# Value products laid out by a table, with six exponentials kept and operands of four head duos

## The chip, the core and the metric

The kernel runs on one core of one Trainium2 chip. The metric is the device time of one execution in microseconds (us), lower is better. The five engines of the core run their own instruction lists in order and wait for each other by semaphores: TensorE (PE in the profile; PEld is its weight load), VectorE (DVE), ScalarE (ACT), GpSimd (POOL) and SyncE (SP, whose queue here only issues DMAs).

## What is computed

Two transformer blocks over x of 8 batches, 1024 rows and 128 channels. Block 0 has one attention head over 1024 rows and a mixture of 8 experts; block 1 has 16 heads of 8 channels and a feed-forward of 512. The change touches the attention of block 1 alone:

```python
def _L1_attn_ref(x, Wq, Wk, Wv, Wout, bout):
    HEADS = 16
    b, n, c = x.shape
    m = HEADS
    d = Wq.shape[0] // m
    q = jnp.einsum('bnc,hc->bnh', x, Wq).reshape(b, n, m, d)
    k = jnp.einsum('bnc,hc->bnh', x, Wk).reshape(b, n, m, d)
    v = jnp.einsum('bnc,hc->bnh', x, Wv).reshape(b, n, m, d)
    scale = d ** (-0.25)
    weight = jnp.einsum('bimd,bjmd->bmij', q * scale, k * scale)
    weight = jax.nn.softmax(weight, axis=-1)
    a = jnp.einsum('bmij,bjmd->bimd', weight, v).reshape(b, n, m * d)
    return jnp.einsum('bnh,ch->bnc', a, Wout) + bout
```

Its 8 x 16 tables of 1024 x 1024 weights are the bulk of the work. Everything else (block 0, the projections, the feed-forward) is called side work here.

## The kernel before

**Units.** Heads go in duos (the code's `pair`): 64 duos, 8 a batch. A duo's tables are cut into `UNITS` = 16 units, each two heads x 128 x 512, which fill one of three PSUM buffers (`buffer`, two banks each). Every table is made twice. The max unit (`max_scores`, L652) has queries on the partitions; VectorE takes its row maxima (`row_max`, L1084). The exp unit (`exp_scores`, L662) has keys on the partitions and three more rows of weights that carry the negated row maxima; ScalarE takes its exponential into `p` (`exps`, L858). A value unit (`values`, L678) multiplies `p` by v: four fp32 products into four groups of 32 columns of `pv_psum`, which sums over the 16 units of a duo. Then ScalarE copies `pv_psum` to `o_sb` (`copy_values`, L864), SyncE writes it out (`values_out`, L1359), and the next duo's first value unit may begin.

**Half steps.** A loop over h, the half step, runs on every engine; there are 1024 with exponentials (128 a batch) and 32 ahead of them. In half step h TensorE fills exp unit h, then max unit h + 32 (`2 * LEAD`), then does value unit h - 2 (`VALUES_LAG`), and then the side stages that a planner (`lay_out`) put there. So each half step has one value unit, whatever else it holds:

```python
        for h in range(-2 * LEAD, PAIRS * UNITS + 2):
            if 0 <= h < PAIRS * UNITS:
                exp_scores(h)
            if h + 2 * LEAD < PAIRS * UNITS:
                max_scores(h + 2 * LEAD)
            if 0 <= h - VALUES_LAG < PAIRS * UNITS:
                values(h - VALUES_LAG)
```

**The ring of three buffers.** Exp and max units take the buffers in turn (exp h, max h + 32, exp h + 1, ...). Max unit h + 32 needs the buffer that exponential h - 1 read, and exp unit h needs that which row maximum h + 30 read. A fill therefore waits (`buffer_of`) if ScalarE or VectorE has not finished its unit of the half step or two before.

**Side work.** All side stages of the loop take turns in one PSUM bank, `side_psum`. A stage that fills it waits until ScalarE or VectorE has emptied it of the one before (`empty`). The planner's `WORK` and `ROOM` set how much side work a half step may get; many half steps have none. Stages that go through `tiled` (L444: block 0's `scores` and `times_v`, `moe`, `wg`, `qk1` and others) use groups of 32 columns as the value units do; transposes (L530, L497, L604) use the whole array; exp and max units use two groups of 64 rows.

**Stores in SBUF.** Four buffers `p`, so exponential n waits for value unit n - 4. The operands `q_ops`, `k_ops` have `SLOTS` = 3 slots of `GROUP` = 2 duos; SyncE loads a group 11 half steps (`LOAD_BEFORE`) before its first max unit, 8 DMAs of 96 KB at a time. The first group's `k_ops` come by ScalarE's queue (`fetch_operands(e, 0, 1)`).

Of the kernel before, what the change touches and what calls it, by code (L numbers as in the profile page):

```python
# [11 lines left out]
P = 128  # L12
# [7 lines left out]
BANK = 512  # L20
HALVES = N // BANK
QUARTER = BANK // 2

VALUES_LAG = 2
EPS = 1e-5
# [10 lines left out]
ROW_HALF = 64  # L36
GROUP = 2
GROUPS = HEADS // 2 // GROUP
SLOTS = 3
VW = DH + 1  # L40
# [44 lines left out]
def half_line(half):  # L85
# [10 lines left out]
    for w in range(2):  # L96
# [24 lines left out]
        "moe": 10, "qk1": 11, "v1": 11, "nm": 1, "w2T": 6, "wff_a": 10, "wff": 12, "wout_mm": 11, "channels_b": 6, "ffn": 11}  # L121
ROOM, ROOM_MOST = (13, 4), 18


# [82 lines left out]


class Side:

# [59 lines left out]
masks_out0 masks_out1 masks_in0 masks_in1 hm gexp0 gexp1 gp0 gp1 x2_0 x2_1 parts0 parts1  # L270
max_filled max_done exp_filled exp_done pv_done pv_copied attention_out operands0 operands1 operands2
nm nm_split maxima0 maxima1
# [3 lines left out]
def build(nc, ctx, x_in, Wq0, Wk0, Wvdown, Wvup, Wg, bg, We, be, c0, wmod0,  # L276
          Wq1, Wk1, Wv1, Wout, bout, W1, b1, W2, b2, c1, wmod1, consts, select, out):
    S = {name: ctx.enter_context(nc.semaphore(name)) for name in SEMAPHORES}
    first, plan, last = make_plan()
    side, before_steps = side_table(first, plan, last)  # L280
    unit_order, unit_at = unit_table()

    def sb(name, shape, dt=F32):
        return ctx.enter_context(nc.sbuf_tensor(name, shape, dt))
# [50 lines left out]
    v1 = [sb(f"v1_{i}", [P, T, HEADS, VW]) for i in range(2)]  # L335
    p_sb = [sb(f"p{i}", [P, 2, BANK]) for i in range(4)]
    mx = [sb(f"row_max{i}", [P, 2, T, HALVES]) for i in range(2)]
# [89 lines left out]
    def tensor_program():  # L427
# [238 lines left out]
        def values(n):  # L666
            pair, kb, half = n // (2 * T), n // 2 % T, n % 2
            b, hp = divmod(pair, HEADS // 2)
            if n % (2 * T) == 0:
                pe.wait_ge(S["pv_zero"], 1)  # L670
                pe.wait_ge(S["pv_copied"], pair)
                emptied("v1", b, 1)
                pe.wait_ge(S["v1_ones"], 2)
            pe.wait_ge(S["exp_done"], n + 1)
            for hh in range(2):
                for part in range(2):
                    q = 32 * (2 * hh + part)
                    m = e.matmul(pv_psum[q:q + VW, half * QUARTER:(half + 1) * QUARTER], v1[b % 2][:, kb, 2 * hp + hh, :],  # L678
                                 p_sb[n % 4][:, hh, part * QUARTER:(part + 1) * QUARTER], start=n % UNITS == 0, stop=n % UNITS == UNITS - 1)
            m.then_inc(S["pv_done"], 1)  # L680
# [9 lines left out]
        for h in range(-2 * LEAD, PAIRS * UNITS + 2):  # L690
            if 0 <= h < PAIRS * UNITS:
                exp_scores(h)
            if h + 2 * LEAD < PAIRS * UNITS:
                max_scores(h + 2 * LEAD)
            if 0 <= h - VALUES_LAG < PAIRS * UNITS:
                values(h - VALUES_LAG)
            for name, *at in plan.get(h, ()):
                if name in stages:
                    stages[name](*at)
# [5 lines left out]
    def scalar_program():  # L705
# [148 lines left out]
        def exps(n):  # L854
            if n >= 4:
                act.wait_ge(S["pv_done"], n - 3)
            act.wait_ge(S["exp_filled"], n + 1)
            e.activation(p_sb[n % 4][:, :, :], unit("exp", n)[0][:, :, :], ACT.Exp).then_inc(S["exp_done"], 1)  # L858

# [14 lines left out]
        for h in range(-2 * LEAD, PAIRS * UNITS + 2):  # L874
            if 0 <= h < PAIRS * UNITS:
                exps(h)
            if h > 1 and h % UNITS == 1:
                copy_values(h // UNITS - 1)
            for name, *at in plan.get(h, ()):
# [404 lines left out]
    def sync_program():  # L1284
# [119 lines left out]
        for h in range(-2 * LEAD, PAIRS * UNITS + 2):  # L1404
            g, within = divmod(h + 2 * LEAD + LOAD_BEFORE, UNITS * GROUP)
            if within == 0 and g < B * GROUPS:
                load_operands(g)
            if h > 1 and h % UNITS == 1:
                values_out(h // UNITS - 1)
            for name, *at in plan.get(h, ()):  # L1410
# [39 lines left out]
```

## Time and profile before

| what | value |
|---|---|
| median of 3 runs | 1938.29 us (1933.97 to 1938.5) |
| the profiled execution | 1939.49 us, its span 1938.2 us |
| TensorE busy | 1736.9 us, 90% of the span |
| VectorE busy | 1527.8 us, 79% |
| ScalarE busy | 1371.4 us, 71% |
| GpSimd busy | 742.8 us, 38% |
| loop from the first exp fill to the last | 214.44 to 1900.61 us |

Busy time is what instructions of an engine cover. A matmul's end is modelled, so matmuls of one engine overlap in the rows: the start of a row less the start of the row before is what the first one cost TensorE, and that is how the rows below are read. In them a row merges neighbouring instructions of one form (x2, x8), and the brackets at its end say how long the engine was idle before it and what it waited for.

### The profile page before, as it was taken

What the parts mean: (1) busy time and instruction counts of PE and PEld (TensorE: products, weight loads), DVE (VectorE), ACT (ScalarE), POOL (GpSimd) and SP (SyncE); (2) the same over time, 40 slices, a digit from 0 to 9 for tenths busy, and PEclk for the clock granted to TensorE, in tenths of its full rate; (3) what the DMA queues carried; (4) which work ended last, traced back from release to release, by engine and by line L of the source; (5) the groups of instructions that cost most, each with busy time, mean ns of one, the idle gap of its engine ahead of it and who ended that gap; (6) DMA issues with size and microseconds to landing.
All of it is one profiled execution on the core that took longest, in us unless ns stands there. A gap on an engine that the chain in (4) does not pass through costs nothing.

```text
span 1938.2 us, 57276 instructions
## 1 busy us (share of the span) xinstructions
PE 1736.9 (90%) x24606; PEld 692.3 (36%) x24606; DVE 1527.8 (79%) x2326; ACT 1371.4 (71%) x1826; POOL 742.8 (38%) x1154
## 2 busy tenths in 40 slices
PE   5675789999999999999999999999999999999994
PEld 3542332333433343343433343343433333222222
DVE  5546877888788887889878887889878887899952
ACT  2431467877788777877778777877788777787883
POOL 2451364325644265324744166333753255102011
PEclk8887799999999999999999999999999999999997
DMA  2012021112111222102211131102311121211101
GB/s 64 24 56 88 24 76 53 32 42 77 51 54 33 55 88 61 47 11 84 75 54 32 43 100 35 51 27 57 98 54 31 44 84 33 65 38 46 34 16 39
DMA packets 97325, 100.46 MB, mean 52 GB/s; under 512 B 11088, under 2 KB 81456, under 8 KB 97072
## 3 DMA queue, kind: packets, MB, share of 16 engines
q1 hardware_dynamic: 95224, 94.84, 16.5%
q8 instruction: 193, 3.16, 0.7%
q10 hardware_dynamic: 1848, 1.97, 0.3%
q14 instruction: 60, 0.49, 0.1%
HBM read 61.25 MB, written 34.73 MB: 50 GB/s over the span
## 4 chain that ended last, share of the span: by engine, by line
PE 55%; ACT 14%; DVE 14%; POOL 9%; issue 6%; DMA 1%; SPq 1%; ACTq 0%; POOLq 0%; DVEq 0%
PE pv_psum L678 17%; PE side_psum L444 14%; ACT p L858 9%; PE buffer L662 9%; PE buffer L652 8%; DVE row_max L1084 8%; PE side_psum L530 2%; POOL hm L1203 2%; PE side_psum L497 1%; PE buffer L444 1%; POOL xn_b L1116 1%; DVE st_f L905 1%; ACT o_sb L864 1%; DVE onehot L1022 1%; ACT s L780 1%
## 5 line engine op out<-in xcount | busy, mean ns | idle before, releaser
L1084 DVE TENSOR_REDUCE row_max<-buffer 128x2 f32<-128x1024 f32 x1024 | 1235.8, 1220 | 255.6 <-PE buffer L652 245.2
L858 ACT ACTIVATE p<-buffer 128x1024 f32<-128x1024 f32 x1024 | 1043.9, 1026 | 245.3 <-PE buffer L662 230.3
L678 PE MATMUL pv_psum<-p,v 128*9 128x256 f32 x8192 | 638.7, 384 | 5.2 <-ACT o_sb L864 2.3
L652 PE MATMUL buffer<-k_ops,q_ops 48*128 48x512 bf16 x2048 | 399.9, 388 | 62.1 <-ACT p L858 25.4
L662 PE MATMUL buffer<-q_ops,k_ops 51*128 51x512 bf16 x2048 | 402.7, 390 | 24.2 <-DVE row_max L1084 18.4
L678 PEld LDWEIGHTS pv_psum<-p,v 128*9 128x9 f32 x8192 | 121.7, 88 | 348.1 <-issue 319.6
L662 PEld LDWEIGHTS buffer<-q_ops,k_ops 51*128 51x128 bf16 x2048 | 98.4, 93 | 389.9 <-DVE row_max L1084 200.5
L1216 POOL TENSOR_SCALAR nm_parts<-nm 128x16 bf16<-128x16 f32 x64 | 13.3, 208 | 401.1 <-DVE nm L1033 400.0
L652 PEld LDWEIGHTS buffer<-k_ops,q_ops 48*128 48x128 bf16 x2048 | 99.8, 94 | 186.7 <-ACT p L858 143.8
L1203 POOL TENSOR_TENSOR hm<-masks,hT_f 128x1024 f32<-128x1024 bf16 x64 | 136.9, 2150 | 28.7 <-PE side_psum L444 26.6
L444 PE MATMUL side_psum<-we,hm 128*32 128x128 f32 x3648 | 122.1, 275 | 6.1 <-POOL hm L1203 6.1
L1180 POOL TENSOR_TENSOR s<-s,consts 128x128 f32<-128x128 f32 x64 | 29.4, 459 | 226.2 <-ACT s L774 225.4
L444 PEld LDWEIGHTS side_psum<-we,hm 128*32 128x32 f32 x3648 | 101.0, 111 | 24.3 <-POOL hm L1203 9.1
L1186 POOL TENSOR_SCALAR rest<-s 128x128 f32<-128x128 f32 (+7 forms) x48 | 102.9, 2143 | 4.2
L780 ACT ACTIVATE s<-s,nm 128x256 f32<-128x256 f32 (+3 forms) x64 | 55.3, 864 | 45.8 <-DVE nm L991 33.1
L1108 POOL TENSOR_SCALAR sm_f<-mv_f 128x4 f32<-128x4 f32 x32 | 6.7, 211 | 184.8 <-DVE mv_f L908 184.8
L444 PE MATMUL side_psum<-v,p0T 128*32 128x129 f32 x1944 | 69.6, 276 | 0.8 <-DVE x L996 0.4
L444 PE MATMUL side_psum<-hT,g 128*32 128x512 f32 (+3 forms) x616 | 65.1, 494 | 0.2 <-ACT s L774 0.2
L444 PEld LDWEIGHTS side_psum<-v,p0T 128*32 128x32 f32 x1944 | 56.9, 111 | 16.9 <-ACT p0T L787 1.6
L774 ACT COPY s<-side_psum 128x512 f32<-128x512 f32 (+3 forms) x77 | 36.8, 478 | 27.7 <-PE side_psum L444 27.0
L787 ACT COPY p0T<-side_psum 128x512 f32<-128x512 f32 (+3 forms) x85 | 43.8, 516 | 17.5 <-PE side_psum L530 14.4
L1116 POOL TENSOR_SCALAR xn_f<-x,sm_f 128x128 f32<-128x128 f32 x112 | 54.0, 496 | 4.3 <-POOL sm_f L1110 4.3
(241 smaller groups left out, 1692.0 us busy)
## 6 DMA issues: line engine op xcount, KB each, us to landing
masks<-masks_rows SPq DMA_DIRECT2D x16, 1024.0 KB, 6.0
q_ops<-products SPq DMA_DIRECT2D x128, 96.0 KB
k_ops<-products SPq DMA_DIRECT2D x124, 96.0 KB
products<-q_parts SPq DMA_DIRECT2D x16, 384.0 KB, 2.8
products<-k_parts SPq DMA_DIRECT2D x14, 384.0 KB, 3.1
attention<-o_sb SPq DMA_DIRECT2D x256, 18.0 KB
x<-in_L_attn_inputs SPq DMA_DIRECT2D x8, 512.0 KB, 4.0
products<-q_parts SPq DMA_DIRECT2D x16, 256.0 KB, 3.1
```

Of the source, the lines that this page charges most:

```text
L444: m = e.matmul(out[q:q + COLUMN_TILE, :], weight[:, q:q + COLUMN_TILE], moving, start=start, stop=stop)
L530: m = e.transpose(v[:, j * P:(j + 1) * P], s0[i % 2][:, k * P:(k + 1) * P], ident)
L652: m = e.matmul(buffer[:, hh, :], q_ops[rows_of(hh, K_MAX), slot, of, i * P:(i + 1) * P], k_ops[rows_of(hh, K_MAX), slot, of, halves(half)[ ...
L662: m = e.matmul(buffer[:, hh, :], k_ops[rows_of(hh, K_EXP), slot, of, kb * P:(kb + 1) * P], q_ops[rows_of(hh, K_EXP), slot, of, halves(half ...
L678: m = e.matmul(pv_psum[q:q + VW, half * QUARTER:(half + 1) * QUARTER], v1[b % 2][:, kb, 2 * hp + hh, :], p_sb[n % 4][:, hh, part * QUARTER ...
L780: e.activation(s[:, start:P + n], s[:, start:P + n], ACT.Exp, bias=nm0[:, i:i + 1]).then_inc(S["p0"], 1)
L787: e.copy(p0T[i % 2][:, some[0]:some[-1] + 1, :].rearrange("p k q -> p (k q)"), v[:, 0:len(some) * P]).then_inc(S["side_act"], 1)
L858: e.activation(p_sb[n % 4][:, :, :], unit("exp", n)[0][:, :, :], ACT.Exp).then_inc(S["exp_done"], 1)
L1084: e.tensor_reduce(mx[pair % 2][:, :, i, half], unit("max", n)[0][:, :, :], axis=AX.X, op=ALU.max).then_inc(S["max_done"], 1)
L1116: m = e.tensor_scalar(xn[:, t, :], src[:, t, :], sm[:, 0, t:t + 1], sm[:, 2, t:t + 1], ALU.add, ALU.mult)
L1186: e.tensor_scalar(rest[:, 0:n], s[:, P:P + n], 0.0, NEG, ALU.is_equal, ALU.mult).then_inc(S["masked"], 1)
L1203: e.tensor_tensor(hm[t % 2][:, :, :], masks[:, :, cols], hT_f[:, cols].unsqueeze(1).broadcast_to([C, EXPERTS, P]), op=ALU.mult).then_inc(S ...
```

## The change

The count of value units in a half step is no longer one. A new function, `value_table`, goes over the half steps once with the plan of side work and chooses 0, 1 or 2 value units for each, so that the sum of squares of TensorE's work is least. Its unit of work is four column-tiled products of 128 columns; a value unit counts 2, a change of tiling `SWITCH` = 0.9, and less than `LIGHT` = 4.8 counts as 4.8. Value unit n is done 2 to 5 half steps (`LAG`, `LAG_MOST`) after exponential n. Two units are not put together where the second opens a new duo. The copy of `pv_psum` and its DMAs follow the half step in which a duo's last value unit stands. `p` has six buffers. The operands have 4 slots of one duo each, and SyncE loads one duo (4 DMAs) every 16 half steps. The order of exp units, max units and side stages is unchanged.

The table has 234 half steps without a value unit, 560 with one and 232 with two.

```diff
-VALUES_LAG = 2
+KEPT, LAG, LAG_MOST = 6, 2, 5
-GROUP = 2
+GROUP = 1
-SLOTS = 3
+SLOTS = 4
+SWITCH, LIGHT = 0.9, 4.8
+def side_work(stage):
+    name, *at = stage
+    if name.startswith("times_v"):
+        return work(stage) / 3, True
+    if name == "scores":
+        return chunks(at[1])[at[2]][1] / P, True
+    if name in ("channels", "channels_b", "transpose_p", "w2T"):
+        return 2.3, False
+    if name in ("nm", "onehotT"):
+        return 0.6, True
+    return (4, True) if name.endswith("_a") or name in EMPTIED_BY else (0, True)
+def value_table(plan):
+    total = PAIRS * UNITS
+    best = {0: (0.0, ())}
+    states = []
+    for h in range(total + LAG):
+        some = [side_work(s) for s in plan.get(h, ())]
+        inside, outside = sum(w for w, tiled in some if tiled), sum(w for w, tiled in some if not tiled)
+        new = {}
+        for left, (cost, at) in best.items():
+            for count in range(3):
+                now = left + (h < total) - count
+                done = min(h + 1, total) - now
+                if not max(0, min(LAG, total + LAG - 1 - h)) <= now + max(0, LAG - 1 - h) or now > LAG_MOST or done - count < 0:
+                    continue
+                if count == 2 and (done - 1) % UNITS == 0:
+                    continue
+                load = inside + outside + 2 * count + SWITCH * ((count > 0 or inside > 0) + (outside > 0))
+                sums = cost + max(load, LIGHT) ** 2
+                if now not in new or sums < new[now][0]:
+                    new[now] = (sums, left, count)
...
+    values_at = value_table(plan)
+    copied_at = {h: units[-1] // UNITS for h, units in values_at.items() if units and units[-1] % UNITS == UNITS - 1}
-    p_sb = [sb(f"p{i}", [P, 2, BANK]) for i in range(4)]
+    p_sb = [sb(f"p{i}", [P, 2, BANK]) for i in range(KEPT)]
...
-            if 0 <= h - VALUES_LAG < PAIRS * UNITS:
-                values(h - VALUES_LAG)
+            for n in values_at.get(h, ()):
+                values(n)
...
-            if n >= 4:
-                act.wait_ge(S["pv_done"], n - 3)
+            if n >= KEPT:
+                act.wait_ge(S["pv_done"], n - KEPT + 1)
...
-            if h > 1 and h % UNITS == 1:
-                copy_values(h // UNITS - 1)
+            if h in copied_at:
+                copy_values(copied_at[h])
```

Two places of TensorE's list show it. The first is in batch 3's side work, half steps 252 to 254: three half steps ahead of and with the transposes of `xn_f` (L497, in the changed kernel L553). Before, exp fill, max fill and value unit (L662, L652, L678) repeat in each:

```order
L662 MATMUL buffer<-q_ops,k_ops 128x512 x2
L652 MATMUL buffer<-k_ops,q_ops 128x512 x2
L678 MATMUL pv_psum<-p,v_1 9x256 x4
L662 MATMUL buffer<-q_ops,k_ops 128x512 x2
L652 MATMUL buffer<-k_ops,q_ops 128x512 x2
L678 MATMUL pv_psum<-p,v_1 9x256 x4
L497 MATMUL side_psum<-consts,xn_f 128x128 x4
```

The changed kernel has at the same place (L718 is the exp fill, L708 the max fill, L734 the value unit):

```order
L718 MATMUL buffer<-q_ops,k_ops 128x512 x2
L708 MATMUL buffer<-k_ops,q_ops 128x512 x2
L734 MATMUL pv_psum<-p,v_1 9x256 x8
L718 MATMUL buffer<-q_ops,k_ops 128x512 x2
L708 MATMUL buffer<-k_ops,q_ops 128x512 x2
L553 MATMUL side_psum<-consts,xn_f 128x128 x4
```

The half step without side work has two value units (x8 in place of x4), and the one with the transposes has none.

The second place is some half steps later, where the experts of the same batch begin (`moe_a`, then `moe`; L444). Before:

```order
L662 MATMUL buffer<-q_ops,k_ops 128x512 x2
L652 MATMUL buffer<-k_ops,q_ops 128x512 x2
L678 MATMUL pv_psum<-p,v_0 9x256 x4
L444 MATMUL side_psum<-be,onehotT 32x128 x4
L444 MATMUL side_psum<-we,hm 32x128 x16
L662 MATMUL buffer<-q_ops,k_ops 128x512 x2
L652 MATMUL buffer<-k_ops,q_ops 128x512 x2
L678 MATMUL pv_psum<-p,v_0 9x256 x4
L444 MATMUL side_psum<-we,hm 32x128 x16
```

And in the changed kernel (L500 is what L444 was):

```order
L718 MATMUL buffer<-q_ops,k_ops 128x512 x2
L708 MATMUL buffer<-k_ops,q_ops 128x512 x2
L500 MATMUL side_psum<-be,onehotT 32x128 x4
L500 MATMUL side_psum<-we,hm 32x128 x16
L718 MATMUL buffer<-q_ops,k_ops 128x512 x2
L708 MATMUL buffer<-k_ops,q_ops 128x512 x2
L500 MATMUL side_psum<-we,hm 32x128 x16
```

Both value units between the fills and the side products are gone from here.

The third is ScalarE's list at the end of the front, ahead of the loop: the DMAs of the first `k_ops` behind the last copies. Before:

```order
L787 COPY p0T<-buffer 128x384
L829 COPY v_0<-side_psum 128x64x8
L419 DMA k_ops<-products 48x1x1024 x4
L780 ACTIVATE s_0<-s_0,nm 128x1024
L774 COPY s_1<-side_psum 128x512 x2
```

And in the changed kernel:

```order
L843 COPY p0T<-buffer 128x384
L885 COPY v_0<-side_psum 128x64x8
L475 DMA k_ops<-products 48x1x1024 x2
L836 ACTIVATE s_0<-s_0,nm 128x1024
L830 COPY s_1<-side_psum 128x512 x2
```

Two of the four DMAs have left ScalarE's queue; SyncE issues them with the next duo.

## Rows read from the trace of the kernel before

**Rows 1.** The page: span, busy time, share of the span, instructions

```profile
span 1938.2 us, 57276 instructions
PE 1736.9 (90%) x24606; PEld 692.3 (36%) x24606; DVE 1527.8 (79%) x2326; ACT 1371.4 (71%) x1826; POOL 742.8 (38%) x1154
PEclk8887799999999999999999999999999999999997
```

**Rows 2.** Busy time in batch 2, batch 6 and batch 7's max units

```profile
664.05:886.17 222.12, 209.77 (x3076) 83.70 (x3073) 184.97 (x280) 170.13 (x227) 100.19 (x151) 1.00 0.19 55
1553.38:1744.72 191.34, 181.39 (x2420) 62.95 (x2417) 166.44 (x191) 147.77 (x176) 61.20 (x91) 0.99 0.19 56
1744.72:1868.60 123.88, 119.28 (x1296) 33.76 (x1292) 119.20 (x123) 102.28 (x110) 17.04 (x43) 1.00 0.13 36
```

**Rows 3.** The timeline, three half steps: start us, us, engine, line

```profile
1437.13 0.39 PE L662 MATMUL buffer<-q_ops,k_ops 51*128 51x512 bf16 x2
1437.36 0.38 PE L652 MATMUL buffer<-k_ops,q_ops 48*128 48x512 bf16 x2
1437.62 2.11 ACT L858 ACTIVATE p<-buffer 128x1024 f32<-128x1024 f32 x2
1437.67 0.62 PE L678 MATMUL pv_psum<-p,v 128*9 128x256 f32 x8
1437.78 1.23 DVE L1084 TENSOR_REDUCE row_max<-buffer 128x2 f32<-128x1024 f32 x1 [0.23 <-PE buffer L652]
1438.22 0.39 PE L662 MATMUL buffer<-q_ops,k_ops 51*128 51x512 bf16 x2
1438.70 0.39 PE L652 MATMUL buffer<-k_ops,q_ops 48*128 48x512 bf16 x2
1439.02 0.62 PE L678 MATMUL pv_psum<-p,v 128*9 128x256 f32 x8
1439.57 0.39 PE L662 MATMUL buffer<-q_ops,k_ops 51*128 51x512 bf16 x2
```

**Rows 4.** The timeline of TensorE in three half steps with side work

```profile
1013.43 1.04 PE L444 MATMUL side_psum<-hT,g 128*32 128x512 f32 x8
1014.40 0.39 PE L662 MATMUL buffer<-q_ops,k_ops 51*128 51x512 bf16 x2
...
1014.94 0.62 PE L678 MATMUL pv_psum<-p,v 128*9 128x256 f32 x8
1015.38 0.40 PE L444 MATMUL side_psum<-hT,g 128*32 128x128 f32 x8
...
1016.42 0.62 PE L678 MATMUL pv_psum<-p,v 128*9 128x256 f32 x8
1016.98 0.66 PE L530 MATMUL side_psum<-consts,s 128*128 128x128 f32 x4
1017.56 0.39 PE L662 MATMUL buffer<-q_ops,k_ops 51*128 51x512 bf16 x2
```

**Rows 5.** The first and the last of 1024 exp fills

```profile
214.44 0.64 PE L662 MATMUL buffer<-q_ops,k_ops 51*128 51x512 bf16 x2
...
1900.61 0.39 PE L662 MATMUL buffer<-q_ops,k_ops 51*128 51x512 bf16 x2
```

**Rows 6.** Idle time of TensorE's weight loads ahead of L652, then L662

```profile
  ACT p L858: 169.2, 475
...
  DVE row_max L1084: 218.9, 474
```

**Rows 7.** The timeline where ScalarE copies a side bank between two fills

```profile
1025.54 0.39 PE L662 MATMUL buffer<-q_ops,k_ops 51*128 51x512 bf16 x2
1025.67 0.59 ACT L774 COPY s<-side_psum 128x512 f32<-128x512 f32 x1 [0.18 <-PE side_psum L444]
1026.16 1.03 ACT L858 ACTIVATE p<-buffer 128x1024 f32<-128x1024 f32 x1
1026.51 0.61 PE L444 MATMUL side_psum<-hT,g 128*32 128x256 f32 x8
```

**Rows 8.** The timeline where the loop begins: ScalarE's queue and TensorE

```profile
158.24 3.71 ACTq L419 DMA_DIRECT2D k_ops<-products  x4
167.49 1.46 PE L652 MATMUL buffer<-k_ops,q_ops 48*128 48x512 bf16 x6 [18.84 <-DMA k_ops<-products]
```

**Rows 9.** Who waited for the copy of `pv_psum` to `o_sb`

```profile
  PEld pv_psum L678: 24.0, 55
```

More of the change, by code:

```diff
@@ L206, in make_plan @@
     return [s for h in sorted(first) for s in first[h]], plan, [(s[0], B - 1, *s[1:]) for gap, s in BACK_LINE]
+def side_work(stage):
[29 more added lines that the diff above has]
+                    new[now] = (sums, left, count)
+        states.append(new)
+        best = {now: (entry[0], ()) for now, entry in new.items()}
+    table, now = {}, 0
+    for h in range(total + LAG - 1, -1, -1):
+        _, left, count = states[h][now]
+        table[h], now = count, left
+    done = 0
+    for h in range(total + LAG):
+        table[h], done = range(done, done + table[h]), done + table[h]
+    assert done == total
+    return table
 class Side:
@@ L270 @@
 masks_out0 masks_out1 masks_in0 masks_in1 hm gexp0 gexp1 gp0 gp1 x2_0 x2_1 parts0 parts1
-max_filled max_done exp_filled exp_done pv_done pv_copied attention_out operands0 operands1 operands2
+max_filled max_done exp_filled exp_done pv_done pv_copied attention_out operands0 operands1 operands2 operands3
 nm nm_split maxima0 maxima1
@@ L678, in values @@
                     m = e.matmul(pv_psum[q:q + VW, half * QUARTER:(half + 1) * QUARTER], v1[b % 2][:, kb, 2 * hp + hh, :],
-                                 p_sb[n % 4][:, hh, part * QUARTER:(part + 1) * QUARTER], start=n % UNITS == 0, stop=n % UNITS == UNITS - 1)
+                                 p_sb[n % KEPT][:, hh, part * QUARTER:(part + 1) * QUARTER], start=n % UNITS == 0, stop=n % UNITS == UNITS - 1)
             m.then_inc(S["pv_done"], 1)
@@ L854, in exps @@
         def exps(n):
-            if n >= 4:
-                act.wait_ge(S["pv_done"], n - 3)
+            if n >= KEPT:
+                act.wait_ge(S["pv_done"], n - KEPT + 1)
             act.wait_ge(S["exp_filled"], n + 1)
-            e.activation(p_sb[n % 4][:, :, :], unit("exp", n)[0][:, :, :], ACT.Exp).then_inc(S["exp_done"], 1)
+            e.activation(p_sb[n % KEPT][:, :, :], unit("exp", n)[0][:, :, :], ACT.Exp).then_inc(S["exp_done"], 1)
         def copy_values(pair):
@@ L1407, in sync_program @@
                 load_operands(g)
-            if h > 1 and h % UNITS == 1:
-                values_out(h // UNITS - 1)
+            if h in copied_at:
+                values_out(copied_at[h])
             for name, *at in plan.get(h, ()):
```

## The prediction

> **What bounds the kernel now.** I read the page first: TensorE is busy 90% of the span, VectorE 79%, ScalarE 71%, and the granted clock is at nine tenths or more from an eighth of the span to its last slice [rows 1]. Then the busy times by stretch [rows 2]. In batch 2, where all side work of the next batches is spread over the half steps, TensorE covers 209.8 of 222.1 us and VectorE 185.0; in batch 6, where there is less side work, VectorE covers 166.4 of 191.3; and in batch 7, as long as there are max units, 119.2 of 123.9. So TensorE sets the end in batches 0 to 5, and VectorE does from the middle of batch 6 on. From the first exp fill to the last the loop takes 1686 us, 1.65 us a half step [rows 5].
>
> Then the timeline, to see what a half step costs TensorE when nothing waits. Starts less starts [rows 3]: exp fill to max fill 0.23, max fill to value unit 0.31, value unit to the next exp fill 0.55, together 1.09 us. With side work [rows 4]: a value unit followed by column-tiled products costs 0.44 (I use 0.43, which the cleanest give), one followed by transposes 0.56; a full column-tiled side product takes 0.97 and four transposes 0.58. So the value unit itself is 0.43, and 0.12 is lost when the tiling changes after it.
>
> Last, the waits. In the second half step of [rows 3] the max fill starts 0.48 after the exp fill and not 0.23: the exponential of the half step before began at 1437.62, takes 1.03, and frees the buffer only then. A half step of 1.09 is shorter than fill, exponential and signal together (about 1.5). The view of who waits puts 169 us of idle weight loads ahead of the max fill down to ScalarE, and 219 us ahead of the exp fill to VectorE [rows 6], but most of that lies under running matmuls. I therefore took the start-to-start distances over the whole loop, between the two fills of [rows 5]. Exp fill to max fill exceeds 0.23 by 97 us in sum over the 992 half steps that have both, and 71 us of these fall in the 397 half steps that come right after one without side work. The 425 half steps without side work last 1.22 us on average (520 us), not 1.09. The 598 others last 1.95 (1166 us). That is the unevenness that the change works on: a short half step runs into a wait, a long one leaves ScalarE and VectorE idle.
>
> **The change, part by part.** I take the counts from the table. Of the 232 value units that leave a half step, 184 leave one with column-tiled side products and 48 leave one with transposes. Of the 232 that come as a second unit, 184 go to half steps without side work, 37 to those with the small `nm` product and 11 to short `scores`.
>
> 1. TensorE's own work. 184 x 0.43 = 79.1 us and 48 x 0.55 = 26.4 us leave; 232 x 0.43 = 99.8 us are added. Net 5.7 us less. The pair "max fill, transposes" stands in no row; its change of tiling lies between 0 (then 0.08 more is saved each, 4 us in all) and the 0.31 less 0.23 of [rows 3], which I take.
> 2. Waits that the second unit fills. A half step of 1.09 + 0.43 = 1.52 us is as long as fill, exponential and signal, so the max fill after it should find its buffer free. Summed over the 228 half steps that get a second unit and are followed by a max fill, with at most 0.43 counted each, that wait is 53 us now; waits of the following exp fill on VectorE add 10. Together 63 us less if all of it is filled. The lower end is half of it, 31, since a wait may only move to the next fill; the upper end is 97 + 10, all such waits.
> 3. New waits after a half step that lost its unit. I compared, for each of the 229 of them ahead of the loop's last max fill, when ScalarE and VectorE were done with the buffer now needed and when TensorE would come if it were 0.43 earlier. 56 come too early, by 12 us in sum. The likeliest are half steps with transposes alone (0.23 + 0.31 + 0.58 = 1.12 us). Bounds: 12, and 40 if every one of the 232 waits 0.17.
> 4. The one side bank. 101 of the half steps without a value unit start a new fill of `side_psum` right after a half step that filled it. Until now the value unit lay between. In [rows 7] ScalarE's copy of the bank begins 0.13 after the next exp fill and gives way 0.49 later, so the bank is free 0.6 to 0.7 after that fill, and the next side product stood 0.97 after it. Without the value unit TensorE is there at 0.54. That is 0.15 each, 15 us; between 5 (after `nm` the copy is short) and 43 (0.43 each).
> 5. The start. TensorE's first max fill waits 18.84 us for the first `k_ops`, whose four DMAs ScalarE's queue takes 3.71 us to issue [rows 8]. Two of them go. 1.9 us less, between 0 and 4.
> 6. At nothing: the loads of operands by one duo. As many DMAs are issued as before; a duo's four take some 3.7 us of the queue (3.71 for four in [rows 8]) and have 11 half steps, 18 us at 1.65, to be issued and to land. If that cover is gone, each duo's first max fill waits. The wait for a slot (the exp units three duos back) was over 22 half steps ahead and is now over 6 ahead. Six `p` buffers never make ScalarE wait, since value unit n - 6 stands ahead of exp fill n. The copy to `o_sb` costs TensorE 24 us now in 55 waits [rows 9]; in 51 of 63 cases the next duo's first value unit is again in the next half step, so this stays. The copy moves by up to 3 half steps, in 18 cases onto a half step where ScalarE also copies a side bank; ScalarE then has 1.03 + 0.59 + 0.59 us of work in a half step of 1.5 to 1.7, 0.3 us late at most, 5 us in all, which I count in the range. Later output DMAs wait for no one: the batch's last copy stays at its half step in all batches but one.
>
> Sum: -5.7 - 63 + 12 + 15 - 1.9 = -43.6 us. The profiled execution took 1939.5 us, 1.2 above the median, so by either the change is from 1938.3 to 1894.7; I say 1895. VectorE's 185 us of a batch then stand in some 215 (86%), and in batches 6 and 7, where VectorE sets the pace, little changes: only 25 of the 184 second units in half steps without side work and 5 of the 53 us of item 2 lie there.
>
> A rule that bears on item 1: the Trainium skill says that changing the tiling mode drains TensorE (TensorEngine Tiling (Array Packing), section Key Properties). By that rule alone a half step that loses its value unit would save two changes, 0.20 us by [rows 3], in all 232 cases, 46 us beside the net of the units. The rows say that a value unit ahead of column-tiled products makes no change of its own (0.44, [rows 4]), so only the 48 with transposes save one, 5.7 us. The rule and the trace agree on what a change costs at all: 0.08 into the value unit and 0.12 out of it.
>
> **The rivals.**
> - VectorE keeps the pace. A row maximum is 1.23 us [rows 3], and VectorE has 1.45 us of work a half step in batch 2. If what the second unit fills comes back as a wait for VectorE in the long half steps, which are now shorter, half of item 2 is lost: -5.7 - 31 + 12 + 15 - 1.9 = -11.6, 1927. For it: 83% busy in batch 2. Against it: 17% is still idle there, and 219 us of [rows 6] lie under matmuls.
> - More than I count. If all waits of the ring go (item 2 at 107) with items 3 and 4 as above: -88, about 1851; if half of the difference comes, 1873. For it: evening out helps later half steps as well.
> - Slower, by the side bank and ScalarE. In a half step without a value unit ScalarE has 1.03 + 0.59 us and two gaps of about 0.1, 1.8 in all, and TensorE 0.23 + 0.31 + 0.97 = 1.51 with full side products [rows 3, 4, 7]. If ScalarE sets the length there, the saved 0.43 is lost in each. The change turns slower when the 232 half steps lose 0.30 us each (69 us by items 1 and 2). At 0.35 each the time is 1938.3 - 69 + 81 = 1950. Against it: ScalarE is ahead in the long half steps, and half steps with a copy every time do not follow each other; in [rows 7] it needs 0.49 before the next exponential begins.
> - No effect: item 2 at 31 and item 3 at 22, so that waits only change places: -5.7 - 31 + 22 + 15 - 1.9 = -1.6, 1937.
>
> **How the numbers follow.** My forecast, 1880 to 1912, has 0.55; VectorE's pace (1912 to 1932) 0.20; more than I count (below 1880) 0.12; no effect 0.06; slower by the side bank 0.07. 0.3% (5.8 us) is about what a measurement of this kernel can tell from no change. Faster by more than that: 0.87, within it 0.06, slower 0.07. The range for 8 in 10 goes from 1868 to 1926; it takes in the lower end of item 2 and half way to its upper end.
>
> **What would show it.** In the changed profile: exp fill to max fill 0.23 after half steps with two value units, and a sum of excess near 45 us in place of 97; two value units 0.43 + 0.55 apart from the next fill; a side product 0.31 after the max fill in half steps without a value unit, but 0.4 to 0.5 where the bank was filled just before; batches 1 to 5 at 214 to 216 us each in place of 222, batch 7 unchanged within 3 us; the first max fill some 2 us earlier. The prediction is wrong if the batches get no shorter with the waits for `row_max` grown, if the idle time ahead of side products grows by over 40 us, or if the max fills after two-unit half steps still wait.

## The result and the profile after

The changed kernel takes 1889.88 us (median of 4 runs, 1886.7 to 1890.62), the kernel before 1938.39 (4 runs): ratio 0.9744, 95% interval 0.9716 to 0.9773. That is 48.5 us less; the forecast was 43.3 less, 1895. A second measurement gave 0.9749 (0.9734 to 0.9765).

The page of the changed kernel, beside [rows 1]:

```profile
span 1889.3 us, 57302 instructions
PE 1706.6 (90%) x24606; PEld 695.4 (37%) x24606; DVE 1522.1 (81%) x2326; ACT 1370.6 (73%) x1826; POOL 741.4 (39%) x1154
PEclk8887799999999999999999999999999999999996
```

The engines do the same work in less time, at the same granted clock. Batch 2 and batch 6, to be held against the first two of [rows 2]:

```profile
644.30:859.40 215.10, 205.99 (x3075) 84.08 (x3071) 184.50 (x281) 170.10 (x227) 99.99 (x151) 1.00 0.19 57
1506.00:1690.80 184.80, 177.79 (x2414) 63.07 (x2410) 166.47 (x192) 147.89 (x176) 61.12 (x91) 1.00 0.19 58
```

Batch 2 went from 222.1 to 215.1 us, batch 6 from 191.3 to 184.8. Three half steps in a row with two value units, none of them with side work:

```profile
885.98 0.39 PE L718 MATMUL buffer<-q_ops,k_ops 51*128 51x512 bf16 x2
886.21 0.38 PE L708 MATMUL buffer<-k_ops,q_ops 48*128 48x512 bf16 x2
886.52 1.05 PE L734 MATMUL pv_psum<-p,v 128*9 128x256 f32 x16
887.50 0.39 PE L718 MATMUL buffer<-q_ops,k_ops 51*128 51x512 bf16 x2
887.73 0.38 PE L708 MATMUL buffer<-k_ops,q_ops 48*128 48x512 bf16 x2
888.04 1.05 PE L734 MATMUL pv_psum<-p,v 128*9 128x256 f32 x16
889.03 0.39 PE L718 MATMUL buffer<-q_ops,k_ops 51*128 51x512 bf16 x2
```

Exp fill to max fill is 0.23 each time, max fill to value units 0.31, value units to the next exp fill 0.98 (0.43 + 0.55): 1.52 us and no wait, as forecast. The half step with transposes that lost its unit, a little later:

```profile
890.35 0.39 PE L718 MATMUL buffer<-q_ops,k_ops 51*128 51x512 bf16 x2
890.73 0.39 PE L708 MATMUL buffer<-k_ops,q_ops 48*128 48x512 bf16 x2
891.41 0.63 PE L553 MATMUL side_psum<-consts,xn_f 128*128 128x128 f32 x4 [0.30 <-POOL xn_f L1172]
891.98 0.39 PE L718 MATMUL buffer<-q_ops,k_ops 51*128 51x512 bf16 x2
```

Here the transposes stand 0.68 after the max fill and not 0.31, since GpSimd's `xn_f` is not ready: side work that used to have a value unit ahead of it now meets its own input. The view of who waits, for the fills, beside [rows 6] (max fill, then exp fill):

```profile
  ACT p L914: 105.4, 346
...
  DVE row_max L1140: 143.7, 308
```

To see where the 47.2 us of the loop came from (exp fill to exp fill, 1686.2 to 1639.0 us) I read every start-to-start distance as in the prediction and took off what each piece costs where nothing waits (0.23, 0.31, 0.43 a value unit, 0.12 after it, and for each side stage the tenth percentile of its own). What is left are waits, put down to the piece that started late. In us, over the loop (another choice of the undisturbed cost, the tenth percentile of every pair of neighbouring pieces, gives 184 and 145 in sum, so the last column is good to some 5 us):

| kernel | exp fill | max fill | value unit | side product | sum |
|---|---|---|---|---|---|
| before | 42 | 96 | 15 | 37 | 189 |
| changed | 26 | 58 | 13 | 49 | 146 |

### The profile page after: what moved, and what is told of

It is laid out like the page before. It is cut to its first block, busy times and chain, and to the rows that moved or that the text cites. A ratio compares the mean times of both kernels' runs of the same rounds, so it can differ in the third digit from the quotient of the medians.

```text
span 1889.3 us, 57302 instructions
## 1 busy us (share of the span) xinstructions
PE 1706.6 (90%) x24606; PEld 695.4 (37%) x24606; DVE 1522.1 (81%) x2326; ACT 1370.6 (73%) x1826; POOL 741.4 (39%) x1154
## 4 chain that ended last, share of the span: by engine, by line
PE 56%; DVE 14%; ACT 11%; POOL 11%; issue 6%; DMA 1%; ACTq 0%; SPq 0%; POOLq 0%; DVEq 0%
PE pv_psum L734 17%; PE side_psum L500 14%; PE buffer L718 10%; PE buffer L708 8%; DVE row_max L1140 8%; ACT p L914 6%; POOL hm L1259 2%; PE side_psum L586 2%; POOL xn_f L1172 1%; PE buffer L500 1%; ACT s L836 1%; POOL xn_b L1172 1%; PE side_psum L553 1%; POOL sm_f L1166 1%; DVE st_f L961 1%
## 5 line engine op out<-in xcount | busy, mean ns | idle before, releaser
L734 PE MATMUL pv_psum<-p,v 128*9 128x256 f32 x8192 | 593.3, 382 | 6.1 <-ACT o_sb L920 4.7
L708 PE MATMUL buffer<-k_ops,q_ops 48*128 48x512 bf16 x2048 | 397.7, 386 | 40.1 <-DMA k_ops<-products 16.5
L718 PE MATMUL buffer<-q_ops,k_ops 51*128 51x512 bf16 x2048 | 401.2, 388 | 11.4 <-DVE row_max L1140 10.7
L734 PEld LDWEIGHTS pv_psum<-p,v 128*9 128x9 f32 x8192 | 145.7, 89 | 328.9 <-issue 257.1
L718 PEld LDWEIGHTS buffer<-q_ops,k_ops 51*128 51x128 bf16 x2048 | 98.1, 92 | 377.7 <-issue 237.6
L708 PEld LDWEIGHTS buffer<-k_ops,q_ops 48*128 48x128 bf16 x2048 | 99.5, 94 | 134.4 <-ACT p L914 94.1
L500 PE MATMUL side_psum<-we,hm 128*32 128x128 f32 x3648 | 122.5, 276 | 5.6 <-POOL hm L1259 5.6
L500 PEld LDWEIGHTS side_psum<-we,hm 128*32 128x32 f32 x3648 | 99.5, 111 | 23.5 <-POOL hm L1259 7.5
L500 PE MATMUL side_psum<-v,p0T 128*32 128x129 f32 x1944 | 70.9, 279 | 0.8 <-DVE x L1052 0.4
L500 PE MATMUL side_psum<-hT,g 128*32 128x512 f32 (+3 forms) x616 | 65.8, 499 | 1.0 <-ACT s L830 0.2
L500 PEld LDWEIGHTS side_psum<-v,p0T 128*32 128x32 f32 x1944 | 53.3, 111 | 23.5 <-issue 12.5
L586 PE MATMUL side_psum<-consts,s 128*128 128x128 f32 x283 | 49.6, 290 | 7.6 <-ACT s L836 3.1
L1045 DVE CUSTOM_DVE_ANT_0 s<-s,rest 128x128 f32<-128x128 f32 (+3 forms) x64 | 49.9, 780 | 4.1 <-POOL rest L1242 3.5
```

The costliest lines, as they stand in the source:

```text
L500: m = e.matmul(out[q:q + COLUMN_TILE, :], weight[:, q:q + COLUMN_TILE], moving, start=start, stop=stop)
L586: m = e.transpose(v[:, j * P:(j + 1) * P], s0[i % 2][:, k * P:(k + 1) * P], ident)
L708: m = e.matmul(buffer[:, hh, :], q_ops[rows_of(hh, K_MAX), slot, of, i * P:(i + 1) * P], k_ops[rows_of(hh, K_MAX), slot, of, halves(half)[ ...
L718: m = e.matmul(buffer[:, hh, :], k_ops[rows_of(hh, K_EXP), slot, of, kb * P:(kb + 1) * P], q_ops[rows_of(hh, K_EXP), slot, of, halves(half ...
L1045: after(e.tensor_tensor_reduce(out=s[:, P:P + n], in0=s[:, P:P + n], in1=rest[:, 0:n], scale=1.0, scalar=NEG, op0=ALU.add, op1=ALU.max, ac ...
```

## The experiments

**Storage alone.** Six `p` buffers and slots of one duo, with the old order.

```diff
-    values_at = value_table(plan)
+    values_at = {h: range(h - LAG, h - LAG + 1) for h in range(LAG, PAIRS * UNITS + LAG)}
```

> The stores of the changed kernel (six p buffers, operands in four slots of one duo), but the old order: one value unit in each half step, two behind its exponential. My theory: the stores by themselves give only the earlier start, 3 us (the first max fill came at 164.2 and not 167.5), so 1935 to 1936; all waits of the loop stay as before (exp fill to max fill 97 us over 0.23 in sum). Rival: the kernel gains because ScalarE has more room in p or the operands come sooner; then this one has a good part of the 48 us, say 1915 or less.

Measured: 1929.02 us, ratio 0.995 (0.9933 to 0.9968), so 9 us of the 48 and not 3. The first exp fill comes 3.2 us earlier (214.4 to 211.3), and the loop is 7.8 us shorter. Half of that is visible: the kernel before had three waits for the rows of maxima, the two largest here.

```profile
557.01 0.39 PE L662 MATMUL buffer<-q_ops,k_ops 51*128 51x512 bf16 x2 [1.54 <-DMA q_ops<-nm_rows]
...
1662.33 0.39 PE L662 MATMUL buffer<-q_ops,k_ops 51*128 51x512 bf16 x2 [2.17 <-DMA q_ops<-nm_rows]
```

SyncE's queue ahead of the second of them, in the kernel before:

```profile
1648.43 1.57 SPq L412 DMA_DIRECT2D products<-q_parts  x3
1650.04 3.43 SPq L419 DMA_DIRECT2D q_ops<-products  x4
1653.51 2.91 SPq L419 DMA_DIRECT2D k_ops<-products  x4
1656.46 1.84 SPq L412 DMA_DIRECT2D products<-k_parts  x3
1658.34 1.73 SPq L1347 DMA_DIRECT2D q_ops<-nm_rows  x2
```

and in this kernel:

```profile
1641.85 1.57 SPq L468 DMA_DIRECT2D products<-q_parts  x3
1643.46 1.52 SPq L475 DMA_DIRECT2D q_ops<-products  x2
1645.02 1.43 SPq L475 DMA_DIRECT2D k_ops<-products  x2
1646.50 1.64 SPq L468 DMA_DIRECT2D products<-k_parts  x3
1648.18 2.15 SPq L1403 DMA_DIRECT2D q_ops<-nm_rows  x2
```

The rows of maxima stand behind the load of operands in one queue; with half the load they go out 9.9 - 6.3 = 3.6 us sooner, counted from the first of `q_parts`, and all three waits (4.3 us) are gone. Where the other 3.5 us of the loop come from the runs do not show, and no run has one of the two stores without the other. The rival, storage as the main cause, is out: the loop is 39 us shorter with the table than with the stores alone (1678.4 to 1639.0).

**The table turned round, and a blind one.**

```diff
-                sums = cost + max(load, LIGHT) ** 2
+                sums = cost - max(load, LIGHT) ** 2
```

> The table with its aim turned round: the sum of squares is made the largest. 313 half steps without side work have no value unit, 112 have two; 398 with side work have two. Theory of even half steps: half steps without side work and value unit are 0.46 us of TensorE's work and still last what VectorE needs, so nothing is saved there, while the others grow: 1990, between 1965 and 2015. Rival, by changes of tiling: 313 x 0.63 + 157 x 0.43 + 42 x 0.55 = 288 us leave TensorE and 510 x 0.43 = 219 us come, 69 us less work than before, so 1870. If tiling is what counted, this is the fastest kernel of all.

```diff
-    values_at = value_table(plan)
+    values_at = {h: range(h - 3, h - 1) for h in range(3, PAIRS * UNITS + LAG, 2)}
```

> None, two, none, two value units in turn, whatever side work the half step has. TensorE's work by its rows: 198 x 0.63 + 248 x 0.43 + 68 x 0.55 = 269 us leave, 512 x 0.43 = 220 us come, 49 us less. Theory of even half steps: the pairs without side work last 2.4 us as before since VectorE and the ring hold them, and side work is as uneven as it was: 1935, between 1922 and 1950. Rival (fewer changes of tiling): 1887.

Measured: 2094.61 us for the reversed table and 2012.47 for the blind one, one execution each, against 1937.62 for the kernel before. Both have less work on TensorE and fewer changes of tiling than the kernel before, and are 157 and 75 us slower. So fewer changes of tiling are not what the change lives on, and uneven half steps cost far more than they save. But my own numbers were off too, by 105 and 77 us, both outside the ranges that I had given. The blind kernel shows why. Late in batch 7 there is no side work; two half steps with the fills alone and the pairs of value units between:

```profile
1702.33 0.39 PE L718 MATMUL buffer<-q_ops,k_ops 51*128 51x512 bf16 x2
1702.55 0.38 PE L708 MATMUL buffer<-k_ops,q_ops 48*128 48x512 bf16 x2
1702.77 0.38 PE L718 MATMUL buffer<-q_ops,k_ops 51*128 51x512 bf16 x2
1702.82 1.94 ACT L914 ACTIVATE p<-buffer 128x1024 f32<-128x1024 f32 x2 [0.93 <-PE buffer L718]
1702.98 2.58 DVE L1140 TENSOR_REDUCE row_max<-buffer 128x2 f32<-128x1024 f32 x2 [0.29 <-PE buffer L708]
1703.90 0.39 PE L708 MATMUL buffer<-k_ops,q_ops 48*128 48x512 bf16 x2 [0.74 <-ACT p L914]
1704.22 1.05 PE L734 MATMUL pv_psum<-p,v 128*9 128x256 f32 x16
1705.20 0.39 PE L718 MATMUL buffer<-q_ops,k_ops 51*128 51x512 bf16 x2
```

The max fill of the second half step (1703.90) waits for the exponential whose unit was filled at 1702.33: 1.57 us from one to the other. In the same pair ScalarE and VectorE run dry (0.93 and 0.29 idle before their next units). A pair takes 2.87 us where two even ones took 2.44. I had put these stretches at VectorE's pace, under which a short half step costs nothing; in truth each max fill must stand some 1.5 us behind the exp fill of the half step before. With 0.23 between a half step's two fills this says: **a half step shorter than 1.27 us costs the next max fill the difference.** By a half step's length this means TensorE's own work in it. The 1.27 was set with the first four kernels of this list in sight; for the other five the sum was worked out from their tables before they ran. The first column is that sum, the second what exp fill to max fill exceeds 0.23 by in the trace, in us:

| kernel | by 1.27 us | measured |
|---|---|---|
| before | 96 | 97 |
| changed | 60 | 59 |
| reversed | 293 | 269 |
| blind | 194 | 204 |
| short lag | 71 | 68 |
| no refill | 62 | 61 |
| other aim | 61 | 60 |
| gap between duos | 74 | 76 |
| no floor | 70 | 67 |

The first column hangs on the lengths put in. With lengths read from each trace (the tenth percentile of every pair of neighbouring pieces) 1.27 gives 81, 54, 287, 197, 63, 55, 55, 70 and 67, too little for the kernel before by 15; with 1.29 all nine lie within 11% of the measured column. After a short half step the max fill stands 1.57 us behind the exp fill in the median of each of these traces. So the rule holds, and its constant is known to some 0.03 us.

**The batch's end.** The table puts batch 6's last value unit three half steps later than in all other batches. In the changed kernel VectorE then waits for the sums:

```profile
1703.51 0.58 SPq L1431 DMA_DIRECT2D sums<-attention  x1
...
1705.77 0.95 DVE L1102 RECIPROCAL sums<-sums 128x128 f32<-128x128 f32 x1 [1.84 <-DMA sums<-attention]
```

```diff
+                if h % (UNITS * HEADS // 2) == 1 and h > 1 and done < h - 1:
+                    continue
```

> The changed kernel, but the last duo of every batch must have all its value units done by the second half step of the next batch. In the changed kernel batch 6's last duo is done three half steps later than that, VectorE then waits 1.8 us for the sums' DMA, and duo 56 lasts 23.2 us where it was 20.0. Theory: 3 us less than the changed kernel, 1887, and no wait of VectorE for the sums within the loop. Rival: duo 56 is longer because VectorE sets the pace there and two-unit half steps hinder it; then 1890 as before.

Measured: 1888.62 us, ratio 0.9743 (0.9728 to 0.9757). In the trace the wait is gone, duo 56 lasts 20.5 us and not 23.2, and the loop is 1635.4 and not 1639.0. The ratio alone, against 0.9744 and 0.9749, cannot tell the two kernels apart.

**Less lag.** To tell the next three kernels from the changed one, it ran once more with them.

> The changed kernel itself once more, on the chip of the next three, so that they can be told from it: 1890, ratio to the kernel before 0.975.

Measured: 1890.69 us, ratio 0.9749 (0.9734 to 0.9765), and the loop to 0.2 us as before (1639.2).

```diff
-KEPT, LAG, LAG_MOST = 6, 2, 5
+KEPT, LAG, LAG_MOST = 4, 2, 3
```

> The changed kernel with four p buffers and a lag of 2 or 3 half steps (179 half steps with two value units instead of 232). The rule that the runs so far gave, that a half step shorter than 1.27 us costs the next max fill the difference, with TensorE's own work and 0.12 us for each new fill of the side bank right behind another in a half step without value unit, gives 1546 us for the changed kernel's loop and 1553 for this one: 7 us slower than the changed kernel, 1897. Rival (every moved unit is worth the same, 39 us for 232): 9 us slower, 1899. The rival that ScalarE needs the six buffers for itself would put it above 1905.

Measured: 1895.86 us, ratio 0.9784 (0.9765 to 0.9803). As forecast by either of the first two; the last rival is out. With four `p` buffers the table gives all but 5 to 7 us of the gain (by the medians and by the ratios).

**Two tables with another aim.** In the first ("no refill" in the tables) leaving out a value unit between two fills of the side bank is so dear (`BANK_COST` = 1000) that the table never does. In the second ("other aim") the aim is the work with a floor, not its square; this one also has the rule on the batch's end.

```diff
-SWITCH, LIGHT = 0.9, 4.8
+SWITCH, LIGHT, BANK_COST = 0.9, 4.8, 1000
...
-                sums = cost + max(load, LIGHT) ** 2
+                sums = cost + max(load, LIGHT) ** 2 + BANK_COST * (count == 0 and fills(h) and filled(h - 1))
```

> The changed kernel, but the table may not leave out the value unit where a side stage fills the side bank right after a half step that filled it (101 such half steps become none; 191 half steps without value unit in all). Rule: 3.6 us more of own work, 2 us more of waits at max fills, 12 us less of waits for the side bank: 6 us faster than the changed kernel, 1884. Rival (the even lengths are what counts; the sum of squares of half-step lengths grows by a fifth of what the change took off it): 8 us slower, 1898.

```diff
-SWITCH, LIGHT = 0.9, 4.8
+SWITCH, LIGHT, BANK_COST = 0.9, 4.0, 0.7
...
-                sums = cost + max(load, LIGHT) ** 2
+                sums = cost + max(load, LIGHT) + 0.01 * load ** 2 + BANK_COST * (count == 0 and fills(h) and filled(h - 1))
```

> The table with another aim: the sum of TensorE's work with a floor of 1.28 us a half step (not of squares; a hundredth of the squares only to choose between equals), 0.15 us for a fill right behind another without a value unit between, and no late batch end. Rule: 1538 us for the loop and not 1546, 8 us faster than the changed kernel, 3 of it for the batch end come on top if that term is real: 1879 to 1882. Rival (VectorE needs even half steps above the floor too, which the squares gave): no faster than 1890.

Measured: 1893.97 us (ratio 0.9769, 0.9753 to 0.9785) and 1897.58 (0.9785, 0.9768 to 0.9802). Both forecasts by my rule (1884, and 1879 to 1882) fall: neither table beats the changed kernel, though the first is not clearly slower either (0.9749, 0.9734 to 0.9765). The trace of the first shows why (it is of the slowest of its five executions, 1898.43): the 14.6 us of waits at the 101 refills (fills of the side bank right after a half step that filled it) are gone, yet waits ahead of side products are 48 us as before, because others came in their place (table below). A wait for the side bank's turn, when removed, is taken up by the next link of the side chain.

**No floor.**

```diff
-SWITCH, LIGHT = 0.9, 4.8
+SWITCH, LIGHT = 0.9, 0.0
```

together with the rule on the batch's end.

> The changed kernel with no late batch end and LIGHT = 0: the plain sum of squares of the half steps' work, without a floor. By the rule of 1.27 us (own work 12 us less, waits at max fills 10 us more, 34 more fills right behind another) it is 1 us slower than the run with the batch end: 1889. By evenness (sum of squares 2187 in place of 2210 us squared, at the 39 us per 98 between storage alone and the change) 9 us faster: 1880. The two runs before spoke for evenness.

Measured: 1898.94 us, ratio 0.978 (0.9766 to 0.9794). Neither: with the least sum of squares of all it is 7 us (by the ratios) to 10 us (by the medians) slower than the same table with the floor. TensorE has 9.5 us less work of its own here, and 22 us more of waits: 9 at max fills, as the rule on 1.27 us says, and 13 ahead of the other pieces, which no number of mine covers.

**A gap between duos.**

```diff
-        for left, (cost, at) in best.items():
-            for count in range(3):
+        for (left, ended), (cost, at) in best.items():
+            for count in range(1 if ended else 3):
...
+                to = now, count > 0 and done % UNITS == 0
```

This one, too, has the rule on the batch's end.

> The changed kernel with no late batch end (as the run of that name), and a duo's first value unit may not stand in the half step right after the last duo's last, so that ScalarE has a whole half step for the copy of pv_psum. The page puts 27 us of waits down to that copy, but the start-to-start distances ahead of value units hold only 13 us of waits of all kinds. Theory: these 10 to 13 us go, and 25 value units are now left out of half steps without side work, which costs 13 us of waits at max fills: 1887 to 1892, no better than 1888.6. Rival (27 us of real waits): 1870.

Measured: 1892.94 us, ratio 0.9754 (0.9741 to 0.9767), just above my 1887 to 1892 and far from 1870. Waits ahead of value units fell from 12 to 5.5 us, those at max fills rose from 57 to 75. The 27 us that the page gives to the copy of `pv_psum` are mostly time that TensorE's matmuls cover.

**VectorE's pace.**

```diff
-            e.tensor_reduce(mx[pair % 2][:, :, i, half], unit("max", n)[0][:, :, :], axis=AX.X
+            e.tensor_reduce(mx[pair % 2][:, :, i, half], unit("max", n)[0][:, :, 0:BANK // 2], axis=AX.X
```

> The changed kernel, but VectorE takes each row maximum over the first 256 of 512 columns only, which halves its largest instruction (1.22 us). The softmax is then shifted by another number. What is left are the waits that are not VectorE's. Theory: the waits ahead of exp fills (26 us) and some ahead of side products go, those ahead of max fills (58 us) stay, since ScalarE's exponential sets them: 1855 to 1865. Rival (VectorE sets the pace in batches 6 and 7, as my prediction has it): half steps without side work fall from 1.24 to 1.1 there, 30 us more, 1830.

> The same halved row maximum in the kernel before (the softmax is shifted by another number). Theory: 42 us ahead of exp fills go, 96 us ahead of max fills stay: 1890 to 1900. Batches 6 and 7 shrink by under 5 us if ScalarE's chain of fill, exponential and fill holds them, by 30 us if VectorE does.

Measured, one execution each: 1858.67 us (31 less than the changed kernel; 1855 to 1865 was expected) and 1901.57 (38 less than before, and just outside my 1890 to 1900). Batches 2 and 6 of the changed kernel with the halved maxima:

```profile
627.50:839.80 212.30, 205.71 (x3075) 84.41 (x3071) 119.32 (x280) 169.75 (x227) 100.32 (x151) 1.00 0.20 58
1477.10:1660.70 183.60, 177.63 (x2416) 63.04 (x2408) 100.62 (x191) 147.75 (x177) 61.18 (x91) 1.00 0.19 58
```

VectorE is busy 101 us of batch 6 and not 166, and the batch is 1.2 us shorter (in the kernel before 0.4, 191.3 to 190.9). Half steps of batch 6 with one value unit and no side work last 1.24 us in both, where the rival had 1.1. The 96 half steps of batch 7 that still have max units shrink from 128.6 to 126.9 us (in the kernel before 125.3 to 123.2). So VectorE does not set the pace in these two batches, where it is busiest. Its maxima cost more in the batches with much side work: batches 1 to 5 are 3 to 5 us shorter each in either kernel. What goes on in batch 6 is to be seen in the same kernel, in half steps without side work:

```profile
1654.02 2.12 ACT L914 ACTIVATE p<-buffer 128x1024 f32<-128x1024 f32 x2 [0.33 <-PE buffer L718]
1654.62 0.39 PE L718 MATMUL buffer<-q_ops,k_ops 51*128 51x512 bf16 x2
1655.10 0.39 PE L708 MATMUL buffer<-k_ops,q_ops 48*128 48x512 bf16 x2
1655.42 0.62 PE L734 MATMUL pv_psum<-p,v 128*9 128x256 f32 x8
1655.53 0.69 DVE L1140 TENSOR_REDUCE row_max<-buffer 128x2 f32<-128x512 f32 x1 [0.66 <-PE buffer L708]
1655.97 0.39 PE L718 MATMUL buffer<-q_ops,k_ops 51*128 51x512 bf16 x2
1656.19 0.38 PE L708 MATMUL buffer<-k_ops,q_ops 48*128 48x512 bf16 x2
1656.46 2.12 ACT L914 ACTIVATE p<-buffer 128x1024 f32<-128x1024 f32 x2 [0.33 <-PE buffer L718]
1656.51 0.62 PE L734 MATMUL pv_psum<-p,v 128*9 128x256 f32 x8
1656.62 0.69 DVE L1140 TENSOR_REDUCE row_max<-buffer 128x2 f32<-128x512 f32 x1 [0.40 <-PE buffer L708]
1657.06 0.39 PE L718 MATMUL buffer<-q_ops,k_ops 51*128 51x512 bf16 x2
1657.54 0.39 PE L708 MATMUL buffer<-k_ops,q_ops 48*128 48x512 bf16 x2
```

Half steps of 1.35 and 1.09 us take turns, 1.22 on average, though VectorE waits 0.66 and 0.40 in turn before its maxima: after each short one the max fill comes 0.48 behind the exp fill, as in [rows 3], and ScalarE waits 0.33 for its next unit. TensorE and ScalarE pace each other through the ring, with VectorE out of it. That it is the exponential's own length that does this is read from the rows; no run made it shorter. 8.5 us of the gain lie ahead of the first exp fill (202.9 and not 211.4): 5.6 in the 32 half steps that have max units alone, and 2.9 ahead of the first max fill, where nothing that was changed has run. This is how far the front differs between executions.

Waits in the loop by the piece that started late, in us ("no late batch end" is the run of that section):

| kernel | exp fill | max fill | value unit | side product |
|---|---|---|---|---|
| storage alone | 36 | 93 | 16 | 36 |
| changed | 26 | 58 | 13 | 49 |
| no late batch end | 23 | 57 | 12 | 50 |
| short lag | 33 | 67 | 11 | 41 |
| no refill | 30 | 59 | 14 | 48 |
| other aim | 30 | 59 | 15 | 49 |
| no floor | 29 | 66 | 15 | 54 |
| gap between duos | 21 | 75 | 6 | 47 |
| changed, half maxima | 11 | 67 | 12 | 35 |
| before, half maxima | 15 | 106 | 14 | 24 |

## Why the prediction was right, step by step

- **TensorE's own work** (5.7 less). The loop is 47.2 us shorter and its waits are 43.6 less, so 3.6 are left for the work. This is what two large sums leave over (the other choice of costs leaves 7.5), so it says no more than that the term is small. The pair that stood in no row, max fill to transposes, is 0.31, the end I took.
- **Waits filled by the second unit** (63 less). Right. Over the half steps that have two units the next max fill waited 56.5 us and waits 7.0; their other waits ahead of the next piece went from 16.1 to 3.8. Together 61.8.
- **New waits after a half step that lost its unit** (12 more). The max fill after them waited 0.9 us and waits 12.5: 11.6 more.
- **The side bank** (15 more). At the 101 refills 2.7 us became 14.6. The size was right, but the table without refills shows that it is no separate price: without them other side products wait as long.
- **The start** (1.9 less). The first max fill waits 16.52 us and not 18.84, and comes 3.3 earlier. ScalarE's queue is through with its `k_ops` 2.0 us sooner (159.9 and not 161.95), and they land faster for the rest. But only the 2.0 are clearly the change's: the first max fill comes at 161.3 to 165.8 in the other traces with this front, and at 166.0 in the second trace of the old one.

```profile
164.22 1.46 PE L708 MATMUL buffer<-k_ops,q_ops 48*128 48x512 bf16 x6 [16.52 <-DMA k_ops<-products]
```

- **"At nothing: the loads of operands by one duo."** Wrong, and the largest miss: storage alone gives 9 us. I looked whether the operands had time to land, which they have, and not at what stands behind them in SyncE's queue. The rows of maxima do.
- **"The batch's last copy stays at its half step in all batches but one."** I saw the one and priced it at nothing. It cost 3.6 us of the loop (1639.0 to 1635.4 without it), and with it batch 7 is 3.7 us longer than before, where I had it unchanged within 3.
- **"VectorE does from the middle of batch 6 on."** Wrong. It is busy there 87% and then 96% of the time, and halving its maxima changed batch 6 by 1.2 us. That little would change in batch 6 was the forecast: it is 6.5 us shorter, 4.1 of them by storage alone. The table brings 2.4 there and nothing in batch 7 (155.8 us without the late end, 155.9 before), as forecast, but not because VectorE sets the pace: few of the second units lie there. This misreading is also why I expected 1990 and 1935 from the reversed and the blind table. The rival "VectorE keeps the pace", which gave back half of the filled waits to VectorE and stood at 1927, is out by the measured time and because the waits ahead of exp fills fell from 42 to 26 us.
- **The signs.** Batches 1 to 5 last 216.8, 215.1, 215.1, 216.1 and 215.4 us; 214 to 216 was forecast. The excess of exp fill to max fill is 59 us and not near 45: that figure took the 53 us of item 2 off 97 and left out the 12 of item 3, with which it is 56. After a refill the side product stands 0.45 behind the max fill on average, as forecast, but by 48 of 101 that wait, not by all.

The first four terms come out within 1 us of their sum, in part by luck, as the first of them is only known to some 4 us. What separates 1895 from 1890 is storage and start, some 7 us too little, less the 3 us of batch 7: two misses that partly cancel. The drain at a change of tiling that the Trainium skill states (TensorEngine Tiling (Array Packing), section Key Properties) is there at the size of the rows, 0.08 into the column tiling and 0.12 out of it, but the reversed table, with 69 us less of work and changes, was the slowest of all kernels.

What stays open: no aim that I tried beats the table's squares with the floor at 4.8. The rule on 1.27 us gives the waits at max fills within a tenth (with the lengths that I put in); for those ahead of exp fills and side products, 75 us in the changed kernel, I have no rule. My forecasts for "no refill" and "other aim" had the wrong sign, and the one for "no floor" was 10 us short. Nor did even lengths as such decide: "no floor" has the least sum of squares of all. No run was clearly faster than the changed kernel with its full work.

## What to carry to other kernels

Where engines hand buffers round a ring, look for the shortest round (here exp fill, exponential, max fill: 1.5 us) and hold every step of the busiest engine against it: work moved from steps above it to steps below it fills waits that are there anyway. Here that was worth 39 us of 1938, after some 24 us of new waits in the steps that gave the work away. An engine that is busy 96% in a stretch need not set its pace (halving its largest instruction took 2 of 125 us off that stretch); shrink its work in one run before building on it. When a transfer is made smaller or moved, look at what stands behind it in the same queue.

## What I had not expected of the hardware

With VectorE's maxima halved (0.69 us in place of 1.23) and VectorE idle over 40% of the time, half steps with one value unit and no side work still last 1.22 us on average in the rows above, and the wait of the max fills grew by 10 us in both kernels (57.8 to 67 and 96 to 106): part of what the exp fill no longer waits, the max fill does. A view that sums idle weight loads (169 us and 219 us in [rows 6]) overstates such waits about twofold and fivefold, as 96 and 42 us by start-to-start distances show.
